# Edge messages of a graph layer: the order of VectorE's six products within a chunk

## What is computed

```python
xn = _layernorm(x, axis=-1)
f1 = feature1 @ w_f1a @ w_f1b * gate_edge
h1 = segment_sum(xn[src] * f1, dst)          # first messages
f2 = f1 * gate_edge
h2 = segment_sum(xn[src] * f2, dst)          # second messages
```

## Time and profile before

| | us |
|---|---|
| median of 3 runs | 1370.49 |
| lowest and highest run | 1360.37, 1372.3 |
| the profiled execution, its own time | 1373.81 |
| its span, first to last instruction | 1372.0 |
| VectorE busy | 862.3 (63%) |
| GpSimd busy | 692.1 (50%) |
| TensorE busy with matmuls | 1126.4 (82%) |

### The profile page before, as it was taken

How to read it: one execution, slowest core, us unless ns; L and a number is a source line. 1 busy time by engine, 2 the same in 40 slices (tenths; PEclk the granted TensorE clock), 3 DMA queues, 4 the chain that set the end, 5 groups by cost and what they waited for, 6 DMA issues and landing times.

```text
span 1372.0 us, 16838 instructions
## 1 busy us (share of the span) xinstructions
PE 1126.4 (82%) x4834; PEld 699.9 (51%) x4834; DVE 862.3 (63%) x1657; ACT 383.1 (28%) x797; POOL 692.1 (50%) x612
## 2 busy tenths in 40 slices
PE   0897769989888898898979958688798788877695
PEld 0563334444444444444434447566676666766484
DVE  2636556666666666657487674366687577666678
ACT  0423333333333333423212131321221131122151
POOL 0005005777777777777200000677676677766411
PEclk9997769999999999998999955799899999998798
DMA  5304015666766666666310001000100010111102
GB/s 147 110 1 146 0 33 175 185 222 193 222 193 219 190 197 215 214 195 190 118 36 0 0 17 9 5 5 4 35 5 4 4 36 4 5 4 4 3 7 69
DMA packets 110963, 117.37 MB, mean 86 GB/s; under 512 B 35970, under 2 KB 95790, under 8 KB 110926
## 3 DMA queue, kind: packets, MB, share of 16 engines
q1 hardware_dynamic: 86606, 71.01, 17.1%
q0 software_dynamic: 24320, 45.91, 13.3%
HBM read 111.47 MB, written 5.41 MB: 85 GB/s over the span
## 4 chain that ended last, share of the span: by engine, by line
POOL 39%; PE 23%; issue 19%; DVE 10%; DMA 6%; ACT 1%; SPq 1%; POOLq 0%; DVEq 0%; ACTq 0%
POOL high L558 19%; POOL high L589 12%; POOL high L591 8%; PE psum L736 4%; DMA high<-dest_rows,high 3%; PE psum L789 3%; PE psum L642 3%; PE psum L695 2%; DVE x_rows L1672 2%; PE psum L781 2%; PE psum L774 2%; DVE low L1229 2%; PE psum L810 1%; DMA high<-xn_rows,srci 1%; PE psum L722 1%
## 5 line engine op out<-in xcount | busy, mean ns | idle before, releaser
L558 POOL DMA_INDIRECT high<-xn_rows,srci x336 | 374.3, 1114 | 259.4 <-issue 174.1
L736 PE MATMUL psum<-high 128*128 128x512 f32 x672 | 314.5, 621 | 18.6 <-DVE high L1276 18.3
L857 PE MATMUL psum<-xT,high 128*128 (+1 forms) x640 | 178.0, 443 | 75.0 <-ACT high L1078 75.0
L736 PEld LDWEIGHTS psum<-high 128*128 128x128 f32 x672 | 129.8, 199 | 179.3 <-issue 148.5
L589 POOL DMA_INDIRECT high<-source_rows,high x128 | 164.5, 1285 | 96.0 <-issue 52.5
L1269 DVE TENSOR_TENSOR high<-psum,high 128x1024 f32<-128x1024 f32 x96 | 100.2, 1086 | 167.1 <-DMA high<-xn_rows,srci 163.6
L857 PEld LDWEIGHTS psum<-xT,high 128*128 128x128 f32 x640 | 145.9, 231 | 104.4 <-issue 58.9
L591 POOL DMA_INDIRECT high<-dest_rows,high x128 | 136.8, 1068 | 41.9 <-issue 41.9
L1013 ACT ACTIVATE high<-iota,nrel 128x128 f32<-128x128 f32 x336 | 103.4, 390 | 171.4 <-PE psum L736 171.1
L868 PE MATMUL psum<-high 128*125 128x256 f32 x640 | 143.8, 379 | 0.0
L722 PE MATMUL psum<-filter_weights,shared 54*128 54x256 f32 x672 | 102.1, 407 | 35.5 <-DVE high L1269 33.4
(11 more groups left out here) (248 smaller groups left out, 1238.2 us busy)
## 6 DMA issues: line engine op xcount, KB each, us to landing
high<-in_ea SPq DMA_DIRECT2D x48, 896.0 KB, 5.8
high<-xn_rows,srci POOLq DMA_INDIRECT x336
shared<-in_ea SPq DMA_DIRECT2D x48, 108.0 KB
high<-in_w SPq DMA_DIRECT2D x8, 512.0 KB, 4.7
shared<-in_ea SPq DMA_DIRECT2D x48, 81.0 KB
x_rows<-in_x SPq DMA_DIRECT2D x5, 500.0 KB
xn_rows<-low SPq DMA_DIRECT2D x5, 500.0 KB
out_rows<-x_rows SPq DMA_DIRECT2D x5, 500.0 KB
```

The costliest lines, as they stand in the source:

```text
L558: pool.indirect_dma_start(gath[j % DEPTH][:, t, :], None, xn_rows_d, bass.IndirectOffsetOnAxis(ap=srci[:, j, t:t + 1], axis=0)).then_inc(s ...
L736: ins = pe.matmul(bank[w % 2], sel[j % 2][:, t, :], msgs[j % DEPTH][:, t, :], start=(j % 2 == 0 and t == 0), stop=(j % 2 == 1 and t == CT ...
L857: ins = pe.matmul(bank[mm][:, 0:HALF], W1s[e % 2][:, k, P * mm:P * mm + P], xT[:, k, bass.ds(n * NW + h * HALF, HALF)], start=(k == 0), st ...
```

## The change

VectorE's six instructions for a chunk come in another order. Before: P1a P1b, P2a P2b, P3a P3b. After: P1a P2a P3a, then P1b P2b P3b. The instructions, their operands, the semaphores and the counts waited for are the same. No other engine's program is changed.

```diff
                 dve.wait_ge(filters_multiplied, q + 3)
                 for h, ts in enumerate(halves):
                     TT(gath[d][:, ts, :], banks[h], gath[d][:, ts, :], ALU.mult).then_inc(filters_taken, 1)
-                for h, ts in enumerate(halves):
-
                     dve.wait_ge(filters_taken, q * 2 + (h + 3))
                     TT(gath[d][:, ts, :], gath[d][:, ts, :], gate[d][:, ts, :], ALU.mult).then_inc(first_messages_ready, 1)
-                for h, ts in enumerate(halves):
                     dve.wait_ge(first_messages_ready, q * 2 + (h + 1))
                     TT(gate[d][:, ts, :], gath[d][:, ts, :], gate[d][:, ts, :], ALU.mult).then_inc(messages_ready, 1)
```

## The result

The changed kernel takes 1401.15 us in the median (1395.53 to 1405.82, 4 runs), the kernel before 1371.39 (1360.37 to 1383.52, 4 runs). The ratio is 1.023, with a 95% interval of 1.019 to 1.027: slower by 2.3%, 30 us. The forecast was 1365, with a range up to 1380.

The account below looks back on a forecast made before the run. GpSimd's issuing of gathers was taken to set the pace, 10.0 us per chunk. The terms -8.3 + 2.0 + 1.4 + 1.2 - 1.4 = -5.1 us took the median from 1370.5 to about 1365, range 1348 to 1380.

Parts of the forecast that it names:

- (3): TensorE's filters wait for the later P1b; sums end 1.3 to 1.9 us later per chunk, covered in the steady stretch.
- rival D: TensorE's two gaps per chunk become one and its clock falls in many chunks: +5 to +15 us; chance 0.08.
- C: Loop through the buffers closes, GpSimd waits for sums every third chunk: 1391; chance 0.10, shared with an unfavourable locked phase.
- (1): VectorE products waiting for the one just ahead cost 0.12 us more each, 0.5 per chunk, hidden in idle time.
- (2): GpSimd gathers starting during products with both operands in SBUF are stretched 0.18 us less per chunk: -8.3 us in all.
- rival B: Gathers' starts lock to VectorE's, leaving one stop of 0.5 us per chunk: up to -30 us, about 1350; chance 0.12.
- The single terms: Delays or gains at single places outside the covered steady stretch: +2.0, +1.4, +1.2 and -1.4 us.
- the start: First chunks of the message stage: filters of chunk 1 wait for P1b of chunk 0, delaying sums and gathers, +2.0 us.
- The end: Last sums have no filters ahead and start after P3a at 3.8 us instead of 5.3: -1.4 us.
- The waits at two later gathers: Gathers at 263.53 and 653.56 us, already close behind their sums, are delayed: +1.4 and +1.2 us.
- A: VectorE's order has no effect on the gathers' stretch, which stays 1.24 us per chunk: +3.2 us, 1374; chance 0.20.

Follow-up runs that it names:

- filters_after_p2: Kernel before, its VectorE order kept, with TensorE's filters also waiting for P2b (start 4.2 us after P1a's): 1385.14 us against 1373.51, ratio 1.008.
- p1_first: Changed kernel with both P1 first again, then P2a P3a P2b P3b: 1362.91 us against 1373.51 for the kernel before, ratio 0.992.
- p1b_third: Same six VectorE instructions as the changed kernel, ordered P1a P2a P1b P3a P2b P3b: 1431.8 us against 1423.2 for the kernel before, ratio 1.013.
- window_inside_2: Second run of p1_first with the window's addition moved between P2b and P3b in every second chunk: 1354.16 us against 1374.81 for the kernel before, ratio 0.982.
- gap_filler_off: Changed kernel with six dummy TensorE matmuls before the filters of chunks 0, 3, 6 and so on: 1389.59 us against 1374.81 for the kernel before, ratio 1.008.
- filler: Changed kernel with six dummy TensorE matmuls between P1a and the filters in every chunk: 1452.63 us against 1423.2 for the kernel before, ratio 1.024.

## Why the prediction was wrong

**The step that failed** is in (3): "In the steady stretch this is covered", 27.7 us for the loop against 30.0. The loop is the right one, and it took 33.0. Its terms, forecast and in the cycle above: end of the sums 13.2 and 17.35, start 0.8 and 0.79, seven gathers 9.7 and 10.09, landing 4.0 and 4.80. The first is the one that failed. Its 13.2 holds where the clock is high (filters at 4.67, sums' ends at 12.9 to 13.3), and there the loop is covered. But (3) took TensorE's durations at the high clock, and rival D took the clock by itself, with 1.5 us of delay per chunk. The two belong together. A chunk whose gathers land late gives a gap of 3.93 us where it was 2.10; the clock falls; filters and sums take 1.8 and 2.7 us longer; the loop is then longer than GpSimd's pace; the gathers it releases are late again for the third chunk on, and the gap returns. Without these 4.5 us the loop above would be 28.5. The two pairs in filters_after_p2 show the same with a start of 4.2 us: 27.8 and 28.4 us for three chunks at the high clock, 31.3 and 32.0 at the low one. So C and D were one case, to which I gave 0.10 and 0.08. C asked for a landing of 6.3 us; the late chunks of the changed kernel's cycle have 4.8 to 5.6, counted from the last gather's end to P1a, and the clock made up the rest. D asked for a low stretch in many chunks; one in three was enough. The time that D named, 1375 to 1385, was too low, since the cycle keeps itself going.

D also read the trace of before too kindly, "in single chunks only". In ten of its chunks from the sixth on, a gap of 1.8 to 2.7 us stands before filters and sums of 9.3 us and more together, instead of 8.3. Their sums still ended by 14.1 us after P1a, and no gather waited over 0.36 us: the low clock without the late filters made no waits, and in the two high-clock chunks of filters_after_p2 the late filters without the low clock made none either.

**(1), the short waits**, held: 505.94 after 504.68 + 1.23, 0.03 us of gap instead of 0.08 of overlap, covered by VectorE's idle time. p1_first shows that they cost nothing.

**(2), the stretch**: the rule held for the single gathers shown, and its count came within 9 us in every order, with gathers costing 344.5, 354.0, 372.2 and 337.3 us where the count gave about 346, 353, 381 and 333 (315 x 0.947 plus 45 times the stops; p1_first, before, p1b_third, window_inside_2). The term for the change, -8.3, was off: the change shows +0.7. (The recorded working, 0.18 us in 45 chunks, makes -8.1.) The count takes the gathers' starts as spread evenly over P2a. In the locked cycle they are not: the third chunk of each has a gather starting right behind P2a's start (1.98 us at 525.32, P2a from 525.25), and so nearly a full first stop. I had named a locked phase as rival B, with the sign in our favour.

**The single terms**: the start cost 2.9 us (taken 2.0). The end gained: the last sums start 3.8 us after P1a instead of 5.3, as taken. The waits at two later gathers (2.6 taken) became eleven with 28 us net. The range reached 1380, though D, which it was to take in, went to 1385.

**The rivals**: A is refuted by p1_first, p1b_third and window_inside_2. The Trainium skill's "SBUF — State Buffer", section "Who interferes with whom", has both sides: its note, by which tensor_tensor did not hold up descriptor writing, doesn't carry over to these gathers, which also read their indices from SBUF; its sentence on two SBUF inputs against GpSimd instructions that read SBUF agrees with these rows. On the clock the Trainium skill's "TensorE: Matmul & The Clock Gate", section "HAM oscillation — how this bites in real kernels", would have told half of the mechanism: bursts with waits between them that run slow each time. The changed kernel's trace agrees in every third chunk, with 3.78 us for filters of 1.99.

**What stays open**: how the 30 us divide between lateness and clock at a start of 4.65. No run held the clock up throughout without giving TensorE more work, and in the changed kernel no chunk with a gap of over 3.7 us kept the high clock. That the lateness costs next to nothing at the high clock rests on the two pairs in filters_after_p2, on two stretches (370 to 471 us of the changed kernel, 496 to 647 of gap_filler_off), and on the arithmetic of the loop. Also open is why one chunk's gathers land 2 us and another's over 5 us after the last has ended; every cycle begins with a late one.

## What to carry to other kernels

When an engine's read frees a single buffer, place that read ahead of everything that only its own engine waits for: moving P1b behind two products cost more than the earlier P3a could bring, since TensorE took its work in order. A slack worked out at the high clock isn't a slack if the edit also lengthens TensorE's idle gaps: work out the loop once more with filters and sums at the low clock, for the chunk whose data comes last. And where GpSimd issues indirect DMAs beside VectorE, count the stops by laying the gathers' starts over the products: the order of instructions that cost the same made between 337 and 372 us of gathers.

## What the runs showed of the hardware

- An indirect DMA of 128 rows on GpSimd that starts during a VectorE product with two SBUF operands ends 0.81 to 0.82 us after that product does, instead of 0.95 after its own start (506.20 in the changed kernel, 454.75 in p1_first). A product with a PSUM operand doesn't hold it, nor one that begins after it (468.28 in window_inside_2).
- A VectorE product that waits for the one just ahead begins 0.03 to 0.04 us after its end (505.94 behind 504.68 + 1.23); one that waits for an earlier one begins 0.08 us before it (two parts of 1.22 and 0.95 in 2.09).
- TensorE's filters with tiles alternating between the two halves of the partitions take 1.99 us for 14 instructions, while 12 of the same size from one half take 2.86 (filler, 401.00 to 403.86 us).
- After a gap of 3.93 us the same 14 instructions took 3.78 us, and the sums 8.97 instead of 6.28, at a granted clock of 0.64 over both. After gaps of 2.99 us they took 1.96 us once and 3.75 us another time (filters_after_p2).
